# A decoder of six stages on one core: causal scores by row halves, earlier loads, a ring bank exchanged, one-hot products over four banks

## The reference

```python
# part 1: causal attention, 16 heads of 64
q, k, v = (x @ w_q), (x @ w_k), (x @ w_v)          # scaled, split into heads
dot = where(causal, einsum('bqhd,bkhd->bhqk', q, k), -inf)
x = x + einsum('bhqk,bkhd->bqhd', softmax(dot), v) @ w_u + b_u
# part 2: attention in chunks of 64 tokens to ctx_1024, 16 heads of 16
scores = einsum('bnqhd,bnkhd->bnhqk', qh, kh) / 4   # q from x, k and v from the context
x = x + einsum('bnhqk,bnkhd->bnqhd', softmax(scores), vh) @ out_proj_w.T + out_proj_b
# part 3: product keys. 8 heads, two sets of 64 keys, the best 8 of 8x8 sums
idx, scores = top_k(sx[..., :, None] + sy[..., None, :])   # experts of 4096
o = gelu(einsum('bnd,bnhkd->bnhk', inputs, key_in[idx])) * softmax(scores)
x = x + einsum('bnhk,bnhkd->bnd', o, key_out[idx])
```

## Time and profile before

| what | us |
|---|---|
| median of 3 executions | 2176.65 (2174.35 to 2184.87) |
| the profiled execution, its own time | 2172.58 |
| its span | 2170.7 |
| PE busy | 1951.1 (90%) |
| DVE busy | 1337.9 (62%) |
| ACT busy | 673.5 (31%) |
| causal attention, to its last residual | 0 to 390.1 |
| chunked attention, to its last pair's projections | 390.1 to about 560 |
| product keys' loop over pairs | about 668 to 1282 |

### The profile page before, as it was taken

One profiled execution on the slowest core, in us unless ns is written; L12 is line 12 of the kernel. 1 busy time (PEld: TensorE's weight loads), 2 busy tenths in 40 slices (PEclk: granted clock), 3 DMA queues, 4 the chain that ended last, 5 costly groups with the idle time before them and its releaser, 6 DMA issues. The chain is left out here.

```text
span 2170.7 us, 42812 instructions
## 1 busy us (share of the span) xinstructions
PE 1951.1 (90%) x16627; PEld 1634.7 (75%) x16627; DVE 1337.9 (62%) x3573; ACT 673.5 (31%) x1539; POOL 159.4 (7%) x121
## 2 busy tenths in 40 slices
PE   4999999688577999999999977877899999999998
PEld 3887887566356888888888864556788888888887
DVE  3566555366638787777877835764565555555554
ACT  2444435234223113212302204443533323323232
POOL 1000000110100000000000006560100000000000
PEclk9999999889768999999999988998899999999999
DMA  3000000100460000000000011000000000000001
GB/s 119 1 1 0 0 0 1 39 15 10 94 110 1 1 0 0 0 0 0 0 0 0 1 43 54 0 0 25 26 30 16 29 14 29 14 29 14 29 15 39
DMA packets 43181, 43.47 MB, mean 20 GB/s; under 512 B 3906, under 2 KB 42338, under 8 KB 43106
## 3 DMA queue, kind: packets, MB, share of 16 engines
q1 hardware_dynamic: 43106, 42.44, 7.3%
HBM read 40.34 MB, written 2.10 MB: 20 GB/s over the span
## 5 line engine op out<-in xcount | busy, mean ns | idle before, releaser
L2198 PE MATMUL f_out<-f_ko,f_gel 128*128 128x256 f32 x1024 | 243.9, 402 | 6.6 <-DVE f_gel L2355 6.6
L2198 PEld LDWEIGHTS f_out<-f_ko,f_gel 128*128 128x128 f32 x1024 | 207.2, 204 | 38.9 <-DVE f_gel L2355 7.3
L2623 DVE TENSOR_TENSOR m_act_up<-m_silu,m_up 128x512 f32<-128x512 f32 x136 | 93.6, 688 | 213.5 <-PE m_up L600 205.8
L2550 ACT ACTIVATE m_silu<-m_gate 128x512 f32<-128x512 f32 x136 | 81.5, 599 | 271.2 <-PE m_gate L600 271.2
L2609 DVE SCALAR_TENSOR_TENSOR g_x<-m_y,m_combine,g_x 128x256 f32<-128x256 f32 x272 | 118.9, 480 | 51.7 <-PE m_y L600 50.2
L229 ACT ACTIVATE a_prob<-a_score,a_neg_max 128x128 f32<-128x128 f32 x256 | 90.7, 367 | 167.0 <-DVE a_neg_max L219 166.9
L600 PE MATMUL f_act<-f_hT_pair_high,f_kiT_high 128*128 128x256 f32 x384 | 123.3, 321 | 0.3 <-ACT f_gel L2231 0.3
L2185 PEld LDWEIGHTS f_g<-f_col_hot,f_row_hot 64*128 64x128 f16 x4096 | 103.0, 94 | 26.8 <-issue 15.9
L2231 ACT ACTIVATE f_gel<-f_act 128x512 f32<-128x512 f32 x128 | 75.5, 598 | 126.2 <-PE f_act L600 107.7
L2185 PE MATMUL f_g<-f_col_hot,f_row_hot 64*128 64x32 f16 x4096 | 109.5, 176 | 2.8 <-DVE f_gel L2355 1.7
L2355 DVE SCALAR_TENSOR_TENSOR f_gel<-f_g,f_gel 128x512 f32<-128x512 f32 x128 | 87.7, 691 | 37.4 <-PE f_g L2185 34.8
(11 more groups left out here) (373 smaller groups left out, 4965.9 us busy)
## 6 DMA issues: line engine op xcount, KB each, us to landing
f_gel<-in_L_ffn_key_in SPq DMA_DIRECT2D x2, 2048.0 KB, 22.2
f_ko<-in_L_ffn_key_out SPq DMA_DIRECT2D x2, 2048.0 KB, 32.0
g_experts_w<-in_L_ffn_w_gate SPq DMA_DIRECT2D x16, 256.0 KB, 2.8
g_experts_w<-in_L_ffn_w_up SPq DMA_DIRECT2D x16, 256.0 KB, 3.0
g_experts_w<-in_L_ffn_w_down SPq DMA_DIRECT2D x16, 256.0 KB, 3.7
x_ctx<-in_ctx SPq DMA_DIRECT2D x8, 256.0 KB, 2.8
fp_wq_nat<-in_L_ffn_w_q SPq DMA_DIRECT2D x1, 2048.0 KB, 9.3
g_ctx_next<-in_ctx SPq DMA_DIRECT2D x8, 256.0 KB, 2.8
```

The lines of the kernel that those rows point to most:

```text
L2198: last = pe.matmul(out_bank[:, t, :], gel[:, r, t * P:(t + 1) * P], ko[:, r, :], start=(r == 0), stop=(r == R - 1))
L2550: act.activation(silu[:, m, :], gate_bank[m][:, :], ACT.Silu).then_inc(silu_ready[m].sem, 1)
L2623: dve.tensor_tensor(act_up[:, m, :], silu[:, m, :], up_bank[m][:, :], ALU.mult) \
```

## The change

Four things are joined.

1. `HeadAttention` becomes `CausalAttention`: keys stay as they are (kT), and a head's scores are a product over its own 64 rows. The two heads of a 128-row tile write different banks, so the scores take four banks, the mask two products of 256 columns, and the transposed probabilities one bank instead of two. half_mask goes.
2. In the causal stage each weight has its own load semaphore, and its rounding and remainder stand between the first projections. The loads of the chunked stage go into memory of their own (`ChunkedInputs`) and are issued in the causal stage, once all of x is in.
3. In the chunked stage ctx moves from ring bank 0 to bank 1, and xn ahead of the second values product.
4. In the product keys stage odd groups of one-hot products use the two act banks, the 64-row halves q alternate, and groups 0 and 1 of block 1 are issued inside outputs(0), before its products 24 and 28. DVE's residual of block 0 stands between its groups 1 and 2 of block 1.

```diff
+        self.score_bank = [s.ps(f"score{n}", [P, 2, 512]) for n in range(2)]
+        self.probT_bank = s.ps("probT_bank", [P, 512])
...
+        for a in range(2):
+            pe.matmul(self.score_bank[n][:, a, 0:2 * P], ident_bf[:, :], mask_bf[:, :], start=True, stop=False,
                       skip_group_check=True)
-        scores(par, self.score_bank[n], b, g, self.mask is None).then_inc(self.scored.sem, 1)
+        for t in range(2):
+            for a in range(2):
+                rows = slice(64 * a, 64 * a + 64)
+                last = pe.matmul(self.score_bank[n][:, a, t * P:(t + 1) * P], qT[par][rows, 2 * g + t, b * P:(b + 1) * P],
+                                 kT[par][rows, 2 * g + t, b * P:(b + 1) * P], start=False, stop=True,
+                                 skip_group_check=True)
+        last.then_inc(self.scored.sem, 1)
...
         pe.wait_ge(self.normed.sem, self.normed.at(i, u + 1))
-        before = self.probT_ready[u % 2]
-        pe.wait_ge(before.sem, before.at(i, u // 2))
+        pe.wait_ge(self.probT_ready.sem, self.probT_ready.at(i, u))
...
+            sp.wait_ge(x_loaded, 32)
+            load_next(sp)
...
-            pe.wait_ge(loaded, 80)
-            pe.wait_ge(low_ready, 3)
-            produce_all(0)
+            ring.wait_slot(pe, 0, 0)
+            ring.wait_slot(pe, 0, 1)
+            for r in range(2, SLOTS):
+                if r in (2, 6, 10):
+                    pe.wait_ge(low_ready, (r - 2) // 4 + 1)
+                produce(0, r)
...
-        ring = TurnRing(s, (("keys", 0, 1), ("queries", 1, 1), ("values", 0, 1), ("xn", 1, 2), ("ctx", 0, 2)), 2)
+        ring = TurnRing(s, (("keys", 0, 1), ("queries", 1, 1), ("xn", 1, 2), ("values", 0, 1), ("ctx", 1, 2)), 2)
...
+        def weight_bank(m, q):
+            return (g_bank if m % 2 == 0 else act_bank)[q]
...
+                def start_weights(t):
                     n = 2 * i + t
                     pe.wait_ge(hot_ready, n + 1)
                     pe.wait_ge(col_ready.sem, col_ready.at(n, 1))
+                    for q in range(2):
+                        pe.wait_ge(act_used[q].sem, act_used[q].at(i, R // 4))
+                def weight_group(t, m):
+                    n = 2 * i + t
+                    for q in range(2):
+                        if m >= 2:
+                            pe.wait_ge(g_used[q].sem, g_used[q].at(n, m - 1))
+                    for j in range(GT):
+                        for part in range(2):
+                            for q in range(2):
+                                rows = slice(q * HALF, (q + 1) * HALF)
+                                last = pe.matmul(weight_bank(m, q)[:, j * R:(j + 1) * R], row_hot[rows, GT * m + j, :],
+                                                 col_hot[rows, part, GT * m + j, :],
+                                                 start=(part == 0), stop=(part == 1))
...
+                def second_weights(r):
+                    if r == 24:
+                        start_weights(1)
+                        weight_group(1, 0)
+                    if r == 28:
+                        weight_group(1, 1)
```

More of the change, by code:

```diff
@@ L204, in __init__, with head_scores, pe_scores @@
         self.bias_added = s.counting("bias_added", 1)
[L206 removed]
+    def head_scores(self, n):
+        return self.score_bank[n][:, :, 0:2 * P].rearrange("p a (t k) -> p a t k", t=2)
+    def pe_scores(self, pe, i, u, par, qT, kT, first=False):
         b, g, n = u // 4, u % 4, u % 2
@@ L276, in copy_out, with pe_first, on_pe @@
         eng.wait_ge(self.weighted.sem, self.weighted.at(i, (c + 1) * self.chunk_units))
-        dst = self.attnT(c)
-        copy(dst, self.out_bank[:, 0:dst.shape[1]]).then_inc(self.out_ready.sem, 1)
-    def pe_first(self, pe, scores):
-        self.pe_scores(pe, 0, 0, 0, scores, first=True)
-        self.pe_scores(pe, 0, 1, 0, scores, first=True)
-    def on_pe(self, pe, i, par, scores, v_ap, before, after):
+        copy(self.attnT(c), self.out_bank[:, :]).then_inc(self.out_ready.sem, 1)
+    def pe_first(self, pe, qT, kT):
+        self.pe_scores(pe, 0, 0, 0, qT, kT, first=True)
+        self.pe_scores(pe, 0, 1, 0, qT, kT, first=True)
+    def on_pe(self, pe, i, par, qT, kT, v_ap, before, after):
         for u in range(UNITS):
@@ L365, in on_dve, with stage_causal_attention @@
             self.links.end()
-def stage_causal_attention(nc, x, ident, ones_row, ident_bf, mask_bf, half_mask, x_in, w_q, w_k, w_v, w_u, b_u):
+def stage_causal_attention(nc, x, ident, ident_bf, mask_bf, x_in, w_q, w_k, w_v, w_u, b_u, load_next):
     HD = 64
@@ L487, in after @@
                         produce(i + 1, r)
-                att.on_pe(pe, i, par, scores, head_values, before, after)
+                att.on_pe(pe, i, par, qT, kT, head_values, before, after)
                 produce(i + 2, 0)
@@ L588, in after @@
                         before(UNITS)
-                att.on_dve(dve, i, par, before, after)
+                att.on_dve(dve, i, before, after)
                 finish_first(dve, i + 2)
@@ L2178, in weights, with outputs @@
                     pe.wait_ge(col_ready.sem, col_ready.at(n, 1))
[L2179 to L2192 removed]
+                    for q in range(2):
[12 more added lines that the diff above has]
+                                                 start=(part == 0), stop=(part == 1))
+                                if j == GT - 1 and part == 1:
+                                    last.then_inc(g_ready[q].sem, 1)
+                def outputs(t, between):
                     n = 2 * i + t
@@ L2208, in _ @@
                         similarities(i, 1, u - 4)
-                weights(0)
+                start_weights(0)
+                for m in range(GU):
+                    weight_group(0, m)
+                    similarities(i + 1, 0, m)
                 turn_codes(i, 1)
-                outputs(0)
-                weights(1)
-                outputs(1)
+                outputs(0, second_weights)
+                weight_group(1, 2)
+                weight_group(1, 3)
+                pe.wait_ge(out_used[0].sem, out_used[0].at(i, 1))
+                outputs(1, lambda r: None)
         @block.scalar
```

246 lines of the change are left out of this document (108 added, 138 removed).

## The result

The changed kernel takes 2089.19 us (median of 4 runs, 2088.61 to 2091.08), the kernel before took 2180.55 in the runs beside it (2174.35 to 2184.87). The ratio is 0.958, with a 95% interval of 0.9557 to 0.9604: faster by 4.2%. I had forecast 2144, in a range of 2116 to 2164. The direction was right. Between the two profiled executions the gain is 81.3 us where I had 32.5, 2.5 times as large. About half of it comes from the one part that I had forecast as a loss, and so does all that I missed.

What follows compares the result with a forecast made beforehand. PE's instructions were taken to bound the causal loop, with PE nearly always busy in the product keys loop. On 2172.6 us, -14.5 - 11 - 19 + 12 = -32.5 gave 2140, or 2144 for a median; range 2116 to 2164.

Steps and rivals of the forecast that it cites:

- part 4: Product keys stage: about 12 us slower, bounds 5 faster and 25 slower.
- I cost the alternation at nothing: One-hot products of the product keys stage: working on two row halves at once gains nothing, 25 ns a product.
- Rival A: One-hot groups: row halves work side by side, a group takes 0.85 instead of 1.62, 42 us gained, 2102; chance 0.10.
- The clock: Product keys loop: 3 us gained by fewer clock falls in block 1, 4 us taken for falls in block 0.
- the wait of 1.29 at the first group: Product keys block 0: the first group waits for both act banks, 1.25 us, of which 0.6 is new.
- a tail: Product keys block 1: two groups behind outputs(0), then a tail of 1.42 + 0.15 us; block 1 0.5 us longer.
- Part 1: Causal start: PE starts at about 17.7 instead of 30.78; 13.8 us gained, and 0.7 for constants; bounds 11 and 15.
- Part 2: Causal scores: 0.69 instead of 0.86 us, a gain of 0.17 a unit in 64 units, 11 us.
- the single bank: Causal loop: transposes wait for the previous unit's copy from the one probT bank; costed at zero, at worst 6 us.
- Part 3: Chunked stage: 19 us gained, from net 3.3 in the first pass, 11 in 6 pairs and 5 by the clock.

Runs made afterwards that it cites:

- no_alternate: The changed kernel, but in each one-hot group the 32 products of one row half come before the 32 of the other: 2129.19 us, 0.9788.
- same_rows: The changed kernel, but both halves of a one-hot group read rows 0 to 63, the two PSUM banks still alternating: 2148.4 us, 0.9877.
- none_inside: The changed kernel with all four one-hot groups of block 1 behind outputs(0), none inside it: 2111.4 us, 0.9687.
- four_only: The changed kernel with block 1's four groups inside outputs(0), before r = 24, 26, 28, 30, block 0's residual behind the fourth multiplication: 2083.83 us.
- four_and_late_wait: four_only, but block 0's first group no longer waits for the act banks, and group 1 comes ahead of the similarity products: 2075.07 us, 0.9524.
- one_probT: The kernel before with a single probT bank instead of two and nothing else: 2207.66 us, 1.0133.
- alternate_only: The kernel before with the alternation of row halves alone, two banks as before, block 1's groups all behind outputs(0): 2189.87 us, 1.0069.
- late_exp: The changed kernel, but ACT's exponentials of block 1 come after gelu 15 instead of after gelu 13: 2110.83 us, 0.9682.

## Why the prediction was wrong

**The step that failed** is in part 4: "I cost the alternation at nothing". It went from a true row (47 loads seen in a us with the clock at 1.00 and 45 with it at 0.50) to "the array isn't what limits them, and working on two row halves at once has nothing to halve". That something doesn't follow the clock doesn't make it a limit of issue. What the runs show instead is a limit of 25 ns for each row half by itself: alternating (with no_alternate against it) takes 14 ns a product, two banks on the same rows 26, and where another group follows 12.7 and 25. Whether it is the weight load or the product that keeps this distance isn't shown. The price is 0.72 us a group, in 8 groups a pair, most of which DVE hides in the last two. Rival A had this mechanism and nearly this size (0.85 a group, 5.3 us a pair, 42 in all, where no_alternate gives 4.4 a pair at the full clock and 40 in all) and the earlier trace rows spoke for it. I gave it a tenth.

The run same_rows is close to the kernel that I had forecast: the halves alternate, the banks and places are those of the change, and the alternation gains nothing. It took 2148.4 us against my 2144, and a pair 78.5 against my 79 to 80. So this one step carries the miss.

The rule that I leaned on, "TensorE: Matmul & The Clock Gate", "Wait — 56ns, not 53.3ns?" in the Trainium skill (starts never closer than about 25 ns), fails here: 12.7 ns at 750.61. The same page of the Trainium skill, section "The mechanism", says that PE pulls a weight load ahead when it goes to other row groups, so that products on different tiles overlap. The Trainium skill's "TensorEngine Tiling (Array Packing)", "Theoretical Speedup", gives up to 2x for a contraction of 64 or less. The runs agree with both, 1.62 to 0.90 is 1.8x.

**The clock** was the second miss of part 4. I gave 3 us for block 1 and took 4 for falls in block 0. Block 1 gained 8 x 1.52 = 12 us in outputs(1), since its small products, with the wait behind them, now last 3.6 us in a row instead of 7.9. Two runs bear this out: with all four groups in a row outputs(1) took 16.5 (none_inside), with each group alone between products of outputs(0) 14.05 or 14.08 in every pair (four_only). Part of the 12 comes with the alternation: in same_rows, where the stretch is 4.8 us as I had forecast, the clock fell in every outputs(1), which took 15.7, and the gain is 5 us. Block 0 fell in none of the seven pairs that have similarity products. On paper the pieces add up: 12 forecast, less rival A's 42, less the 9 that the forecast didn't have of these 12 and the 4 that weren't lost, is -43, and -43.0 was measured in the loop. But errors cancel in it. By same_rows the change without the overlap costs the loop 8.3 us, not 12 (598.96 against 590.68), and the overlap with its share of the clock brings 51.3. That the same sum for the whole kernel, 2102 - 13 = 2089, hits the measured median too is luck: parts 1 to 3 gave 7 us less than I had forecast, and the changed kernel's median lies 1.9 us below its profiled execution, where I had added 4.

**Right in part 4:** the wait of 1.29 at the first group (1.25 forecast), and that there is a tail, where outputs(1) waits 1.82 instead of 0.83. Both were real costs, and four_and_late_wait cut them to 0.40 and 0.84.

**Part 1** was right: 17.20 against 17.7 forecast, the loop 13.0 us earlier against 13.8 and 0.7.

**Part 2** had the mechanism and missed the size by 5. Mask and scores gained 0.12 instead of 0.17 a unit (3 us), and the single bank, costed at zero with 6 at worst, costs 3.4 by one_probT, some of it at half the clock. In the changed loop PE waits 3.0 and 2.9 us for probT (the copies by DVE and by ACT), of which some would have been other waits: the first seven pairs are 1.06 us shorter each, the last one 1.2 longer. I had looked at units between which projections stand. The last pair has none, and there five of the eight transposes wait, up to 1.7 us.

**Part 3** came out at 17.9 against 19 by two errors that cancel. The pair fell to 16.65, below my 17 to 18.5, since the clock fell in none of the gaps that are left, where I expected two falls. But the first pass lost 7.7 instead of 2.4. Values behind xn are 3.0 of it (398.62 to 412.18 is 13.6; 10.6 before). In the first pass xn and ctx now follow each other into the same bank, the 0.68 at 384.42, which I missed and which is 1.3 with what the clock adds. The remaining 3.4 are the clock: PE is at 1.2 GHz from 375 to 392, 14.6 us into the stage, and again from 395 to 402, where before it was at 2.4 again at 406, 3.4 us in, though the first products are the same. That isn't settled. With the early loads the first stretch lasted until 389.1 to 394.2 in all thirteen profiles; without them it lasted until 406 in two, and until 413 and 419 in the other two (alternate_only, one_probT). The first pass took 34.3 to 35.0 us with the early loads, and 27.0 twice, 32.9 and 31.2 without. So the kernel before may partly have been lucky in its profile.

## What to carry to other kernels

Small products that take nearly the same time at either clock are not at a floor until they have been spread over row groups: count the time for each row half apart, and change the half after four products at the latest. Such a gain arrives only if what empties the results can lag behind, so ask at once how many banks it needs; with two it was lost, with four it was 40 us. And when a rival rests on a row of the same array (here the tiled scores) and the forecast on an inference from another, the rival deserves more than a tenth.

## What the runs showed of the hardware

- One-hot products of 64 rows and 32 columns: 25 ns each on one half (1.62 us for 64 where another group follows, same_rows), 12.7 on alternating halves (0.81, the changed kernel), and 0.08 us where products of another form follow. Each change of half hides three products (0.076 us); one, two or four products a half before it changes all take 0.90 to 0.92 us in 64.
- PE's records interleave across such a border: products of the next group start between the last three of this one (685.39 to 685.43, no_alternate).
- The clock depends on more than the stretch itself: with the same instructions in each of the first seven pairs, outputs(1) of the changed kernel took 14.05 us in four pairs and 15.4 to 15.7 in the other three.
- With 1.29 us of idling ahead of the small products the clock stayed up (the changed kernel); with 0.78 and 1.57 around the first group it fell in five of seven pairs, and the loop took 14 us longer (late_exp).
- A kernel whose product keys code is untouched lost 27 us there, with stalls of 2.2 us on issue and twice the instruction packets (one_probT). A comparison of two kernels should look at these packets before it explains a difference in code that hasn't changed.
